# Output projection and skip sums of a decoder layer in products of rounded parts, on one Trainium2 core

## The chip, the cores and the metric

The kernel runs on one core of a Trainium2 chip. The metric is the device time of one execution in microseconds. Three runs of the kernel before took 540.54, 540.75 and 542.11 us: a median of 540.75.

## What is computed

The input is x, 16 sequences of 128 tokens of 256 features in float32. One decoder layer, with a layer norm behind each of its three parts:

```python
x = layernorm(x + attention(x))   # 16 heads of 16, causal in chunks of 64, RMS norm of o per head, then o @ wo.T
x = layernorm(x + xattn(x, ctx))  # kv = x * ctx per pair of channels; long convolution with k,
                                  # y = conv(kv) + kv * skip, out = sum over i of y * ctx
x = layernorm(x + ffn(x))         # gelu(x Wg) * (x Wu), times Wd; the weights are 4-bit codes with scales
```

In attention, q and k are products of two projections each. `skip` is one number for each of the 128 tokens. The FFN is 2048 wide.

## The kernel before

**Groups.** The 16 sequences are four groups of 512 tokens (g = 0 to 3; the text calls them group one to four). What comes before the FFN, called the front here (attention, convolution, skip sum), is cut into stages; the FFN is 16 tiles of 128 rows. After group one's front, which runs alone, the front of group g runs in between the FFN tiles of group g - 1: in slot s an engine does its part of gate of tile s, then the first stages of the slot, then its part of up, the second stages, its part of down, the third stages. TensorE does down one tile late. The fixed lists `slots` (lines 224 to 236) and `last_slots` for group four (lines 238 to 245) say which stage stands where. Between two groups lies a turn (`turn`, one function for each engine), with the end of one front, the start of the next, and the last layer norm of the group before.

**Order.** Each engine runs its own list in the order in which the schedule writes it, and waits on semaphores (`count`, `wait_ge`). A wait at the head of an engine's list holds up everything behind it on that engine.

**Products of parts.** TensorE takes float32 operands in several passes. Most products are therefore made of parts: a value is rounded to float32r by a copy on ScalarE (`_hi`), VectorE subtracts to get the rest (`_lo`), and `split_mm` (lines 155 to 159) makes three single-pass products of them. The float32 products left in the front are the output projection (`outproj`, line 1290), the convolution (lines 1320 to 1323) and the skip sum (line 1339).

**Attention's end.** Slot 5 gives the RMS (`sums`, `rms`); slot 6 ends with ScalarE's `wide` (line 644); slot 7 begins with `factor`: TensorE transposes the factors (line 1278), ScalarE copies them (line 651), VectorE multiplies o by them (line 855). Behind that in slot 7 come, on VectorE, `inner` (line 1099, inter = gelu x up) and `split` (line 1088, inter_lo), and on ScalarE `inner_hi` (line 727) between the two. Slot 8 has both halves of `outproj`, one behind gate, one behind up; VectorE adds each half to x (line 883) and takes the statistics. Slot 9 normalises (line 876) and transposes x1 for the convolution. Group four has the same stages one slot earlier.

**Group two** also has the rest of the weight unpacking beside it (`unpack`, lines 766 to 794 on VectorE, 585 to 598 on ScalarE), a piece ahead of `inner` in each of slots 1 to 5 and 7 to 10.

**Convolution and skip sum.** Sixteen `conv` stages end in slot 15. POOL makes kv (line 533) and the products for the skip sum (`skip_products`, line 501, in conv 12 and 14). VectorE gates and sums each convolution one stage later (`conv_sum`, lines 905, 910). In the turn TensorE makes the two skip sums (line 1339, one matrix product each with `skip_mat`, a block matrix that holds the skip factor), transposes the convolution back (line 1351, after `conv_ready`) and starts the next group's projections, whose tokens are split into parts (`split_x`, lines 564 and 739) at the start of the turn. The loads of tokens stand on SP (line 380).

Of the kernel before, what the change touches and what calls it, by code (L numbers as in the profile page):

```python
# [20 lines left out]
P = 128  # L21
# [32 lines left out]
def decoder_layer(nc, x, xT, ctx, ctxT, wq, wk, wvT, woT, fT, bias, skip, toep,  # L54
# [7 lines left out]
    with ExitStack() as stack:  # L62
# [10 lines left out]
        wo_sb = sb("wo_sb", [P, KT, D])  # L73
# [7 lines left out]
        skip_mat = sb("skip_mat", [P, CH, CI])  # L81
        head_sel = sb("head_sel", [P, HT])
# [8 lines left out]
        with ExitStack() as early:  # L91
            def sbe(name, shape, dt=F32):
                return early.enter_context(nc.sbuf_tensor(name, shape, dt))
            wv_sb = sbe("wv_sb", [P, KT, D])
            xT_sb = sbe("xT_sb", [P, KT, T])
            inter = sbe("inter", [P, 2, T])
        wv_lo = sb("wv_lo", [P, KT, D], F32R)
        xT_lo = sb("xT_lo", [P, KT, T], F32R)
        inter_lo = sb("inter_lo", [P, 2, T], F32R)

# [10 lines left out]
        kT_sb = sb("kT_sb", [P, KT, T])  # L111
# [12 lines left out]
        qbd = sb("qbd", [P, 4, T])  # L124
# [51 lines left out]
        shifted, masked, deq_ready, wlo_ready = sems("shifted", "masked", "deq_ready", "wlo_ready")  # L176
        minus_ready, wlo_mm, wlo_act = sems("minus_ready", "wlo_mm", "wlo_act")
# [9 lines left out]
        last_mm, last_stored = sems("last_mm", "last_stored")  # L187
        end_inter, end_hi, end_lo = sems("end_inter", "end_hi", "end_lo")
# [8 lines left out]
        weight = sb("weight", [P, 2, 2, QC])  # L197
# [33 lines left out]
        slots[7] = [("factor", 0), pause, pause]  # L231
# [327 lines left out]
        def _(act):  # L559
# [20 lines left out]
            act.wait_ge(filled, 6)  # L580
            act.wait_ge(bd_ready, 1)
# [57 lines left out]

            def wide(g, _):  # L640

                count(act, ms_mm, 2, g, 2)
                count(act, rms_ready, 1, g, 1)
                nc.scalar.activation(rms_sb[:].rearrange("p k (n e) -> p (k n) e", e=DK),
                                     inv_rms[:].unsqueeze(2).broadcast_to([P, NB * H, DK]), ACT.Copy)\
                    .then_inc(wide_ready, 1)

            def factor(g, _):
                count(act, rT_mm, 2, g, 2)
                for mt in range(KT):  # L650
                    nc.scalar.activation(by_seq(fac_sb, mt), factor_part(mt), ACT.Copy).then_inc(rT_ready, 1)

# [12 lines left out]
            def conv(g, h):  # L665

                if h + NTOEP - 1 < CH:
                    load_filter(g, h + NTOEP - 1)

# [13 lines left out]
            def turn(done, prev, g, beside=nothing):  # L683
# [8 lines left out]
                if g is not None:  # L692
                    if g:
                        split_x(g)
# [21 lines left out]
            def inner_hi(g, n):  # L716
# [8 lines left out]
                if n >= 2:  # L725
# [4 lines left out]
                                 "norm": norm, "conv": conv},  # L730
# [4 lines left out]
        def _(dve):  # L735
# [26 lines left out]
            dve.wait_ge(const_ready, 4)  # L762
            nc.vector.tensor_scalar(skip_mat[:], skip_mat[:], skip_sb[:, 0:1], None, ALU.mult).then_inc(dve_const, 1)
# [59 lines left out]

            def rms(g, _):
# [26 lines left out]
            def factor(g, _):  # L851
                count(dve, o_mm, NU_S, g, NU_S)
                count(dve, rT_ready, 2, g, 2)
                for mt in range(KT):
                    nc.vector.tensor_tensor(by_seq(o_sb, mt), o_part(mt), by_seq(fac_sb, mt), ALU.mult)\
                        .then_inc(on_ready, 1)

# [32 lines left out]
            def conv(g, h):  # L890

                if h:
                    conv_sum(g, h - 1)
                if g == 0 and h == CH - 1:
# [94 lines left out]
            def turn(done, prev, g, beside=nothing):  # L989
# [8 lines left out]
                if g is not None:  # L998
                    if not isinstance(g, int) or g:
                        split_x(g)  # L1000
# [100 lines left out]
            def finish():  # L1101
# [17 lines left out]
                for b in range(NB):  # L1119
# [3 lines left out]

            schedule(dve, turn, {"score": score, "squares": squares, "rms": rms, "factor": factor, "outproj": outproj, "norm": norm,
                                 "conv": conv, "join": join, "norm2": norm2, "late": late}, nothing, inner, split, unpack, finish)


        @block.tensor
        def _(pe):
# [154 lines left out]
            def outproj(g, j):  # L1284
                if isinstance(g, int) and g == 0:
                    pe.wait_ge(dve_const, 8)
                count(pe, on_ready, 2, g, 2)
                for b in (2 * j, 2 * j + 1):
# [43 lines left out]
            def skip(g, j):  # L1332
# [4 lines left out]
                    elif g == 0 and j:  # L1337
                        pe.wait_ge(z_ready, CH - 1)
                    nc.tensor.matmul(skip_bank(g, j)[:, :], skip_mat[:].rearrange("p h i -> p (h i)"), prod_sb[:, j, :],
# [171 lines left out]
```

## Time and profile before

| | |
|---|---|
| median of three runs | 540.75 us |
| the profiled execution | 540.84 us, its span 539.0 us |
| TensorE busy | 521.3 us, 97% of the span |
| VectorE busy | 369.4 us, 69% |
| ScalarE, POOL busy | 153.2 us (28%), 125.6 us (23%) |
| mean granted TensorE clock | 0.996 |
| chain that ended last | TensorE 84%, VectorE 9%, issue 3% |

Times on the time lines are microseconds from the start of the span. PE is TensorE, PEld its weight loads, DVE VectorE, ACT ScalarE. A row "x8" is several records in one; a float32 product leaves two records. A duration holds the latency, and the next instruction of the engine can start before it is over: the pitch from start to start is what an engine needs for one. A few records are missing. A bracket at the end of a row is the time that the engine sat idle before it, and who ended that.

### The profile page before, as it was taken

To read this page: it belongs to the slowest core of one execution; us is meant where nothing else is said; L and a number is where in the kernel's file an instruction comes from. 1 tells how busy PE (TensorE), PEld (TensorE's weight loads), DVE (VectorE), ACT (ScalarE), POOL (GpSimd) and SP (SyncE) were. 2 spreads that over 40 slices of the span, in tenths; PEclk is the share of its full clock that TensorE was granted. 3 is DMA by queue.
4 is the path that set the end of the run, shared out by engine and by line. 5 is a ranking of instruction groups with operands and counts; after the bars stand their busy time and mean duration, and the time that the engine had idled before them with its cause. 6 is when DMAs were issued, how large, how long until landed. Compare 5 with 4: busy or idle time off the path is not lost.

```text
span 539.0 us, 8767 instructions
## 1 busy us (share of the span) xinstructions
PE 521.3 (97%) x3335; PEld 424.2 (79%) x3335; DVE 369.4 (69%) x774; ACT 153.2 (28%) x277; POOL 125.6 (23%) x194
## 2 busy tenths in 40 slices
PE   8999899899999999999999999999999999999994
PEld 8746676667888888867888888866888888888883
DVE  5998989878595678865454768875464777743335
ACT  4564300333422112331333111241332101333230
POOL 3000198210014452220004444120013570100001
PEclk9999999999999999999999999999999999999998
DMA  5662321401111110050001110040001210010001
GB/s 158 170 184 79 88 78 52 136 21 49 51 29 29 52 49 1 0 193 5 1 1 49 50 50 11 1 152 6 1 1 49 69 40 1 2 39 1 1 0 39
DMA packets 25256, 26.80 MB, mean 50 GB/s; under 512 B 2816, under 2 KB 22784, under 8 KB 25216
## 3 DMA queue, kind: packets, MB, share of 16 engines
q1 hardware_dynamic: 14752, 16.26, 9.8%
q10 hardware_dynamic: 10032, 8.43, 5.4%
q0 software_dynamic: 432, 1.57, 0.8%
q8 instruction: 26, 0.43, 0.3%
q14 instruction: 14, 0.11, 0.1%
HBM read 24.15 MB, written 2.10 MB: 49 GB/s over the span
## 4 chain that ended last, share of the span: by engine, by line
PE 84%; DVE 9%; issue 3%; DMA 1%; POOL 1%; ACT 1%; POOLq 0%; DVEq 0%; SPq 0%; ACTq 0%
PE bank L1157 17%; PE bank L1158 16%; PE bank L1159 16%; PE front_bank L1320 5%; PE front_bank L1323 5%; PE front_bank L1321 5%; PE front_bank L1228 3%; PE front_bank L1214 3%; PE front_bank L1157 2%; PE front_bank L1159 2%; PE front_bank L1158 2%; PE front_bank L1290 2%; DMA raw_s<-in_up_s 1%; PE front_bank L1263 1%; DVE st L864 1%
## 5 line engine op out<-in xcount | busy, mean ns | idle before, releaser
L1157 PE MATMUL bank<-x2T_lo,ffn_hi 128*128 128x512 f32 x256 | 109.7, 429 | 1.4 <-DVE x2T_lo L1043 1.4
L1158 PE MATMUL bank<-x2T_hi,ffn_lo 128*128 128x512 f32 x256 | 100.7, 393 | 0.0
L1159 PE MATMUL bank<-x2T_hi,ffn_hi 128*128 128x512 f32 x256 | 100.7, 393 | 0.0
L1099 DVE TENSOR_TENSOR inter<-bank,inter 128x512 f32<-128x512 f32 x63 | 43.5, 691 | 82.6 <-PE bank L1159 82.4
L533 POOL TENSOR_TENSOR qbd<-qT_sb,ctxT_sb 128x256 f32<-128x256 f32 x128 | 79.4, 643 | 67.5 <-PE front_bank L1323 54.0
L474 POOL TENSOR_TENSOR ve<-ve,minus_half 128x2 f32<-128x2 f32 x24 | 18.4, 766 | 306.9 <-DVE ve L869 248.5
L727 ACT ACTIVATE inter_hi<-inter 128x512 fp32r<-128x512 f32 x63 | 39.8, 632 | 145.5 <-DVE inter L1099 145.5
L1157 PE MATMUL bank<-ffn_lo,inter_hi 128*128 128x256 f32 x256 | 76.3, 298 | 1.2 <-DVE inter_lo L1088 0.9
L714 ACT ACTIVATE inter<-bank 128x512 f32<-128x512 f32 x64 | 38.2, 597 | 128.5 <-PE bank L1159 128.5
L1158 PE MATMUL bank<-ffn_hi,inter_lo 128*128 128x256 f32 x256 | 71.6, 280 | 0.0
L1159 PE MATMUL bank<-ffn_hi,inter_hi 128*128 128x256 f32 x256 | 71.1, 278 | 0.0
L1088 DVE TENSOR_TENSOR inter_lo<-inter,inter_hi 128x512 fp32r<-128x512 f32 x63 | 47.4, 753 | 23.2 <-ACT inter_hi L727 17.5
L1157 PEld LDWEIGHTS bank<-x2T_lo,ffn_hi 128*128 128x128 f32 x256 | 48.1, 188 | 15.6 <-issue 8.0
L1159 PEld LDWEIGHTS bank<-x2T_hi,ffn_hi 128*128 128x128 f32 x256 | 48.1, 188 | 11.1
L1158 PEld LDWEIGHTS bank<-x2T_hi,ffn_lo 128*128 128x128 f32 x256 | 48.3, 189 | 7.8 <-issue 0.2
L814 DVE TENSOR_TENSOR gate_q<-front_bank,causal 128x1024 f32<-128x1024 f32 x32 | 39.1, 1222 | 20.7 <-PE front_bank L1228 20.7
L1157 PEld LDWEIGHTS bank<-ffn_lo,inter_hi 128*128 128x128 f32 x256 | 48.2, 188 | 6.4 <-issue 4.2
L905 DVE TENSOR_TENSOR qbd<-front_bank,ctxT_sb 128x256 f32<-128x256 f32 x128 | 47.8, 415 | 3.7 <-PE front_bank L1323 3.3
L1158 PEld LDWEIGHTS bank<-ffn_hi,inter_lo 128*128 128x128 f32 x256 | 48.1, 188 | 1.8
L1159 PEld LDWEIGHTS bank<-ffn_hi,inter_hi 128*128 128x128 f32 x256 | 48.0, 188 | 0.0
L910 DVE TENSOR_REDUCE gate_q<-qbd 128x64 f32<-128x512 f32 x64 | 43.9, 686 | 2.2
L1320 PE MATMUL front_bank<-qbd,toep_sb 128*128 128x256 f32 x128 | 39.1, 387 | 2.6 <-POOL qbd L533 1.9
(145 smaller groups left out, 775.0 us busy)
## 6 DMA issues: line engine op xcount, KB each, us to landing
toep_sb<-in_toep ACTq DMA_DIRECT2D x64, 128.0 KB, 2.1
xT_sb<-in_xT SPq DMA_DIRECT2D x4, 512.0 KB, 5.5
ctxT_sb<-in_ctxT SPq DMA_DIRECT2D x4, 512.0 KB, 4.8
x_sb<-in_x SPq DMA_DIRECT2D x4, 512.0 KB, 6.0
ctx_sb<-in_ctx SPq DMA_DIRECT2D x4, 512.0 KB, 6.9
out<-ctxT_sb POOLq DMA_DIRECT2D x3, 512.0 KB, 3.4
raw_w<-in_gate_p SPq DMA_DIRECT2D x8, 128.0 KB
raw_s<-in_gate_s SPq DMA_DIRECT2D x8, 128.0 KB
```

The source lines that it names most:

```text
L533: nc.gpsimd.tensor_tensor(pairs(kv_sb, h % 2)[:, kt], v_i, c_j, ALU.mult).then_inc(kv_ready, 1)
L714: nc.scalar.activation(inter[:, n % 2, :], gate_ps[:, :], ACT.Gelu_apprx_tanh).then_inc(gelu_ready, 1)
L727: nc.scalar.activation(inter_hi[:, n % 2, :], inter[:, n % 2, :], ACT.Copy).then_inc(ihi_ready, 1)
L814: nc.vector.tensor_tensor(sc_sb.rearrange("p (r k) c -> p r k c", k=2), front_ps[:, :, 0:2 * P].rearrange("p r (k c) -> p r k c", c=P), ca ...
L905: last = nc.vector.tensor_tensor(pairs(z_sb, h % 2)[:, lt], fb[h % 2][:, :].rearrange("p (k b j i) -> p k b j i", k=KT, b=NB, i=CI)[:, lt] ...
L910: nc.vector.tensor_reduce(conv_sb[:, :, :, h * CI:(h + 1) * CI], pairs(z_sb, h % 2), AX.X, ALU.add)\
L1088: nc.vector.tensor_tensor(inter_lo[:, n % 2, :], inter[:, n % 2, :], inter_hi[:, n % 2, :].bitcast(F32), ALU.subtract).then_inc(ilo_ready, 1)
L1099: nc.vector.tensor_tensor(inter[:, n % 2, :], up_ps[:, :], inter[:, n % 2, :], ALU.mult).then_inc(inter_ready, 1)
L1157: nc.tensor.matmul(ps, w_hi, x_lo, start=start, stop=False, skip_group_check=True)
L1158: nc.tensor.matmul(ps, w_lo, x_hi, start=False, stop=False, skip_group_check=True)
L1159: return nc.tensor.matmul(ps, w_hi, x_hi, start=False, stop=stop, skip_group_check=True)
L1320: nc.tensor.matmul(fb[h % 2][:, 0:n], diag, kv[:, 0:n], start=True, stop=True)
```

## The change

1. In groups two to four, `outproj` uses three single-pass products of parts for each float32 product. wo is split once: ScalarE rounds it at the end of slot 6 of group two, ahead of `wide`, and VectorE subtracts in slot 7. o is split for each group: ScalarE's `round_o` stands in slot 7 behind up, VectorE's `split_o` in slot 7 behind down. TensorE waits for both halves of o_lo (and once for wo_lo).
2. In groups two and three each skip sum is two single-pass products with a matrix of ones and zeros (`skip_ones`, rounded once at the start). ScalarE scales by skip and rounds (`prod_hi`) in conv 13 and 15, VectorE makes `prod_lo` there.
3. The tokens of groups three and four are split within the slots and not in the turn: ScalarE's half behind the factor copies of slot 7, VectorE's half behind the second half of `outproj` in slot 8.
4. Tiles are laid out anew to make room: o_hi and o_lo lie over qbd, wo_lo over wo_sb, prod_lo over kT_sb, prod_hi over weight.

```diff
@@ -70,7 +70,7 @@
         wv_hi = sb("wv_hi", [P, KT, D], F32R)
-        wo_sb = sb("wo_sb", [P, KT, D])
+        wo_hi = sb("wo_hi", [P, KT, D], F32R)
         ffn_hi = sb("ffn_hi", [P, 3, 2, F], F32R)
@@ -79,6 +79,7 @@
         skip_mat = sb("skip_mat", [P, CH, CI])
+        skip_ones = sb("skip_ones", [P, P], F32R)
         head_sel = sb("head_sel", [P, HT])
@@ -94,9 +95,17 @@
             inter = sbe("inter", [P, 2, T])
+            wo_sb = sbe("wo_sb", [P, KT, D])
+            qbd = sbe("qbd", [P, 4, T])
+            kT_sb = sbe("kT_sb", [P, KT, T])
+            weight = sbe("weight", [P, 2, 2, QC])
         wv_lo = sb("wv_lo", [P, KT, D], F32R)
         inter_lo = sb("inter_lo", [P, 2, T], F32R)
+        wo_lo = sb("wo_lo", [P, KT, D], F32R)
+        o_parts = sb("o_parts", [P, 4, T], F32R)
+        prod_lo = sb("prod_lo", [P, 2, T], F32R)
+        prod_hi = sb("prod_hi", [P, 2, T], F32R)
@@ -108,7 +117,6 @@
         rms_sb = x1T_sb = qT_sb
-        kT_sb = sb("kT_sb", [P, KT, T])
         fac_sb = prod_sb = kT_sb
@@ -121,7 +129,7 @@
-        qbd = sb("qbd", [P, 4, T])
+        o_hi, o_lo = o_parts[:, 0:2, :], o_parts[:, 2:4, :]
         q_two = qbd[:].rearrange("p u (k c) -> p u k c", c=S)
...
@@ -194,7 +204,6 @@
         code_f16 = code[:].bitcast(F16)[:, :, 1::2]
-        weight = sb("weight", [P, 2, 2, QC])
         x2T_hi = sb("x2T_hi", [P, 2, T], F32R)
@@ -228,7 +237,7 @@
         slots[6] = [pause, pause, ("wide", 0)]
-        slots[7] = [("factor", 0), pause, pause]
+        slots[7] = [("factor", 0), ("round_o", 0), ("split_o", 0)]
         slots[8] = [("outproj", 0), ("outproj", 1), pause]
@@ -578,6 +587,9 @@
             act.wait_ge(filled, 6)
+            act.wait_ge(const_ready, 2)
+            nc.scalar.activation(skip_ones[:], skip_mat[:].rearrange("p h i -> p (h i)"), ACT.Copy)\
+                .then_inc(ones_rounded, 1)
             act.wait_ge(bd_ready, 1)
@@ -637,8 +649,18 @@
+            def round_o(g, _):
+
+                if g:
+                    for mt in range(KT):
+                        count(act, on_ready, 2, g, mt + 1)
+                        nc.scalar.activation(o_hi[:, mt, :], o_sb[:, mt, :], ACT.Copy).then_inc(ohi_ready, 1)
+
             def wide(g, _):
+                if g == 1:
+                    act.wait_ge(wo_mm, 2)
+                    nc.scalar.activation(wo_hi[:], wo_sb[:], ACT.Copy).then_inc(wohi_ready, 1)
                 count(act, ms_mm, 2, g, 2)
@@ -649,6 +671,8 @@
                     nc.scalar.activation(by_seq(fac_sb, mt), factor_part(mt), ACT.Copy).then_inc(rT_ready, 1)
+                if 0 < g < G - 1:
+                    split_x(g + 1)
@@ -666,6 +690,13 @@
                     load_filter(g, h + NTOEP - 1)
+                if 0 < g < G - 1 and h in (CH - 3, CH - 1):
+                    j = h // 2 + 2 - CH // 2
+                    count(act, prod_ready, 2, g, j + 1)
+                    if j == 0:
+                        act.wait_ge(wlo_ready, NU - NU_S)
+                    nc.scalar.activation(prod_hi[:, j, :], prod_sb[:, j, :], ACT.Copy, scale=skip_sb[:, 0:1])\
+                        .then_inc(phi_ready, 1)
@@ -690,8 +721,6 @@
                 if g is not None:
-                    if g:
-                        split_x(g)
                     for p in range(0, 8, 2):
...
@@ -760,6 +789,7 @@
             dve.wait_ge(const_ready, 4)
+            dve.wait_ge(ones_rounded, 1)
             nc.vector.tensor_scalar(skip_mat[:], skip_mat[:], skip_sb[:, 0:1], None, ALU.mult).then_inc(dve_const, 1)
@@ -821,6 +851,12 @@
+            def outproj_of(g, j):
+
+                outproj(g, j)
+                if j and 0 < g < G - 1:
+                    split_x(g + 1)
+
             def rms(g, _):
@@ -855,6 +891,18 @@
+            def split_o(g, _):
+
+                if g == 1:
+                    dve.wait_ge(wohi_ready, 1)
+                    nc.vector.tensor_tensor(wo_lo[:], wo_sb[:], wo_hi[:].bitcast(F32), ALU.subtract)\
+                        .then_inc(wolo_ready, 1)
+                if g:
+                    for mt in range(KT):
+                        count(dve, ohi_ready, 2, g - 1, mt + 1)
+                        nc.vector.tensor_tensor(o_lo[:, mt, :], o_sb[:, mt, :], o_hi[:, mt, :].bitcast(F32),
+                                                ALU.subtract).then_inc(olo_ready, 1)
+
             def stats(g, ln, tile, j):
@@ -891,6 +939,12 @@
                     conv_sum(g, h - 1)
+                if 0 < g < G - 1 and h in (CH - 3, CH - 1):
+                    j = h // 2 + 2 - CH // 2
+                    count(dve, phi_ready, 2, g - 1, j + 1)
+                    nc.vector.scalar_tensor_tensor(prod_lo[:, j, :], prod_sb[:, j, :], skip_sb[:, 0:1],
+                                                   prod_hi[:, j, :].bitcast(F32), ALU.mult, ALU.subtract)\
+                        .then_inc(plo_ready, 1)
                 if g == 0 and h == CH - 1:
@@ -995,9 +1049,6 @@
                     conv_sum(prev, CH - 1)
-                if g is not None:
-                    if not isinstance(g, int) or g:
-                        split_x(g)
                 if done is not None:
...
@@ -1285,6 +1336,17 @@
                 count(pe, on_ready, 2, g, 2)
+                if g == 1:
+                    pe.wait_ge(wolo_ready, 1)
+                if g:
+                    count(pe, olo_ready, 2, g - 1, 2)
+                    for b in (2 * j, 2 * j + 1):
+                        toks = slice(b * S, (b + 1) * S)
+                        for kt in range(KT):
+                            last = split_mm(fb[j][:, (b % 2) * D:(b % 2 + 1) * D], o_hi[:, kt, toks], o_lo[:, kt, toks],
+                                            wo_hi[:, kt, :], wo_lo[:, kt, :], kt == 0, kt == KT - 1)
+                    last.then_inc(wo_mm, 1)
+                    return
                 for b in (2 * j, 2 * j + 1):
@@ -1336,6 +1398,13 @@
                         pe.wait_ge(z_ready, CH - 1)
+                    if 0 < g < G - 1:
+
+                        count(pe, plo_ready, 2, g - 1, j + 1)
+                        nc.tensor.matmul(skip_bank(g, j)[:, :], skip_ones[:], prod_hi[:, j, :], start=True, stop=False)
+                        nc.tensor.matmul(skip_bank(g, j)[:, :], skip_ones[:], prod_lo[:, j, :], start=False, stop=True)\
+                            .then_inc(skip_mm, 1)
+                        return
                     nc.tensor.matmul(skip_bank(g, j)[:, :], skip_mat[:].rearrange("p h i -> p (h i)"), prod_sb[:, j, :],
```

## Rows read from the trace of the kernel before

**Rows 1.** The page: busy time by engine; costliest groups (busy us, mean ns, idle before).

```profile
PE 521.3 (97%) x3335; PEld 424.2 (79%) x3335; DVE 369.4 (69%) x774; ACT 153.2 (28%) x277; POOL 125.6 (23%) x194
...
L1157 PEld LDWEIGHTS bank<-ffn_lo,inter_hi 128*128 128x128 f32 x256 | 48.2, 188 | 6.4 <-issue 4.2
```

**Rows 2.** TensorE's waits, whole run: releaser: us in total, times, longest us.

```profile
PE front_bank L1320 <- POOL qbd L533: 1.9, 2, 1.5
...
PE front_bank L1157 <- DVE xT_lo L739: 0.3, 1, 0.3
```

**Rows 3.** TensorE's time line, group three's output projection: start, us, engine, line, instruction.

```profile
275.81 1.89 PE L1290 MATMUL front_bank<-wo_sb,gate_q 128*128 128x256 f32 x8
...
277.76 0.39 PE L1158 MATMUL bank<-x2T_hi,ffn_lo 128*128 128x512 f32 x1
...
282.06 0.39 PE L1157 MATMUL bank<-x2T_lo,ffn_hi 128*128 128x512 f32 x1
...
284.85 0.28 PE L1157 MATMUL bank<-ffn_lo,inter_hi 128*128 128x256 f32 x1
...
286.24 1.04 PE L1302 MATMUL front_bank<-ident,x_sb 128*128 128x128 f32 x8
```

**Rows 4.** Time lines of TensorE, VectorE, ScalarE and POOL, turn behind group two's front.

```profile
210.36 1.88 PE L1339 MATMUL bank<-kT_sb,skip_mat 128*128 128x512 f32 x4
212.08 1.04 PE L1351 MATMUL front_bank<-ident,gate_q 128*128 128x128 f32 x8
...
209.14 0.76 DVE L905 TENSOR_TENSOR qbd<-front_bank,ctxT_sb 128x256 f32<-128x256 f32 x2
...
210.53 1.28 DVE L739 TENSOR_TENSOR xT_lo<-xT_sb,xT_hi 128x512 fp32r<-128x512 f32 x2
...
206.41 1.14 ACT L564 ACTIVATE xT_hi<-xT_sb 128x512 fp32r<-128x512 f32 x2
...
204.97 1.27 POOL L501 TENSOR_TENSOR kT_sb<-x_sb,ctx_sb 128x512 f32<-128x512 f32 x1
```

**Rows 5.** Time lines of ScalarE, TensorE and VectorE, slots 6 to 9, group two.

```profile
144.49 1.04 ACT L644 ACTIVATE qT_sb<-inv_rms 128x1024 f32<-128x1024 f32 x1
145.80 1.04 PE L1278 MATMUL front_bank<-ident,qT_sb 128*128 128x128 f32 x8
...
150.83 1.89 PE L1290 MATMUL front_bank<-wo_sb,gate_q 128*128 128x256 f32 x8
...
160.79 0.36 PE L1157 MATMUL bank<-ffn_lo,inter_hi 128*128 128x256 f32 x1 [0.75 <-DVE inter_lo L1088]
...
152.81 0.69 DVE L1088 TENSOR_TENSOR inter_lo<-inter,inter_hi 128x512 fp32r<-128x512 f32 x1 [0.69 <-ACT inter_hi L727]
153.42 0.68 DVE L883 TENSOR_TENSOR x_sb<-front_bank,x_sb 128x512 f32<-128x512 f32 x1
...
155.29 0.51 DVE L774 TENSOR_SCALAR code<-raw_w 128x256 int32<-128x256 int32 x2
...
159.95 0.69 DVE L1088 TENSOR_TENSOR inter_lo<-inter,inter_hi 128x512 fp32r<-128x512 f32 x1
```

**Rows 6.** Time lines of VectorE and ScalarE, slot 7, group three.

```profile
273.03 1.29 DVE L855 TENSOR_TENSOR gate_q<-front_bank,kT_sb 128x512 f32<-128x512 f32 x2 [2.75 <-ACT kT_sb L651]
...
275.62 0.69 DVE L1088 TENSOR_TENSOR inter_lo<-inter,inter_hi 128x512 fp32r<-128x512 f32 x1 [0.70 <-ACT inter_hi L727]
...
274.96 0.63 ACT L727 ACTIVATE inter_hi<-inter 128x512 fp32r<-128x512 f32 x1 [2.02 <-DVE inter L1099]
```

**Rows 7.** Stretch behind group two's projection: busy us, PEclk after POOL's count, DMA, GB/s.

```profile
151.00:157.00 6.00, 6.00 (x34) 5.33 (x34) 5.07 (x14) 1.64 (x3) 0.69 (x1) 1.00 0.00 0
```

**Rows 8.** Time lines of ScalarE and VectorE at the start, of SP's token loads.

```profile
9.85 0.31 ACT L583 ACTIVATE minus_ident<-ident 128x128 fp32r<-128x128 f32 x1
...
10.87 0.28 DVE L763 TENSOR_SCALAR skip_mat<-skip_mat,skip_sb 128x128 f32<-128x128 f32 x1
...
134.17 0.40 SPq L380 DMA_DIRECT2D xT_sb<-in_xT  x1
```

More of the change, by code:

```diff
@@ L176, in decoder_layer @@
         shifted, masked, deq_ready, wlo_ready = sems("shifted", "masked", "deq_ready", "wlo_ready")
+        wohi_ready, wolo_ready, ohi_ready, olo_ready = sems("wohi_ready", "wolo_ready", "ohi_ready", "olo_ready")
         minus_ready, wlo_mm, wlo_act = sems("minus_ready", "wlo_mm", "wlo_act")
@@ L187, in decoder_layer @@
         last_mm, last_stored = sems("last_mm", "last_stored")
+        ones_rounded, phi_ready, plo_ready = sems("ones_rounded", "phi_ready", "plo_ready")
         end_inter, end_hi, end_lo = sems("end_inter", "end_hi", "end_lo")
@@ L729, in _ @@
             schedule(act, turn, {"score": score, "squares": squares, "wide": wide, "factor": factor, "x1T": x1T,
-                                 "norm": norm, "conv": conv},
+                                 "norm": norm, "conv": conv, "round_o": round_o},
                      gelu, inner_hi, nothing, unpack, nothing)
@@ L1122, in finish @@
                                             ALU.subtract, ALU.mult).then_inc(res_ready, 1)
-            schedule(dve, turn, {"score": score, "squares": squares, "rms": rms, "factor": factor, "outproj": outproj, "norm": norm,
-                                 "conv": conv, "join": join, "norm2": norm2, "late": late}, nothing, inner, split, unpack, finish)
+            schedule(dve, turn, {"score": score, "squares": squares, "rms": rms, "factor": factor, "outproj": outproj_of, "norm": norm,
+                                 "conv": conv, "split_o": split_o, "join": join, "norm2": norm2, "late": late}, nothing, inner, split, unpack, finish)
         @block.tensor
```

## The prediction

> **What bounds the kernel now.** I read the page's busy table first: TensorE is busy for 521.3 of 539.0 us, the next engine for 369.4 [rows 1]. Then who TensorE waited for: the list is short, its longest single wait 1.5 us [rows 2], and the same view cut to 164 to 410 us, where most of the changed work lies, lists none. So between those times each microsecond that the change takes out of TensorE's stream shortens the run, and each that TensorE is made to wait lengthens it; nothing gives it back, since TensorE has no idle time to catch up in. The one wait within reach of the change is 0.75 us at 160.79 in group two, where VectorE, not TensorE, is the last to finish: it works without a gap from 153.42 to 159.95 us, in 14 entries, up to the tile that TensorE waits for [rows 5]. Third, the time line around the output projection and the turns, which gives the slack that the new roundings have.
>
> **TensorE's own work.** A half of the output projection (four float32 products of 256 columns) starts at 275.81; the second product behind it starts at 277.76, and one such product takes 0.23, so the half takes 1.72. Twelve single-pass products of 256 columns run from 284.85 to 286.24: 1.39 [rows 3]. The new half is twelve of these: 0.33 less. The Trainium skill (TensorE: Matmul & The Clock Gate, part 3, "What overlaps and what doesn't") says that a weight load overlaps products in flight only when the row groups differ; by that rule each product here would pay its load too, 0.12 + 0.19, a new half would take 3.7 against 1.72 + 8 x 0.19 = 3.2, and the sum below would come to 549.6. The rows contradict it, so it gets no chance: the load takes 188 ns, yet products start every 0.116 us, so it is hidden [rows 1, 3].
>
> Both skip sums of a group take 210.36 to 212.08, 1.72 us [rows 4]. Four single-pass products of 512 columns replace them; twelve take 282.06 to 284.85, so one 0.2325 and four 0.93 [rows 3]. That is 0.79 less per turn, in two turns (groups two and three). Of it some 0.05 is lost: the second prod_lo stands on VectorE before the last conv_sum. Now that conv_sum starts at 209.14; prod_lo's price lies between the pitch of a subtraction, 0.60 (two take 1.28, one 0.69), and its whole duration, 0.69 [rows 4, 5]; at 0.61 plus its 0.05 handover conv_sum ends near 211.3, where TensorE now wants it at 210.36 + 0.93 = 211.29. I take 0.74 per turn, bounds 0.6 and 0.79: **-1.5** in all. The first prod_lo waits for ScalarE, and ScalarE for POOL's product; POOL's second product is done at 206.24, ScalarE comes to it at 206.41 [rows 4], and the first stands one stage earlier, in VectorE's idle time before it multiplies the last FFN tile. Queued behind that ScalarE wait is inter_hi of the tile, and nobody is later for it.
>
> **The new chain in front of the output projection.** In slot 7 ScalarE's queue holds gelu, the factor copies (and now split_x of the next group), inner_hi, then round_o; VectorE's holds the factor products, inner, split, then split_o. So the rounding of o is queued behind inner_hi, though o itself has long been ready. Group three: inner_hi starts at 274.96; a 512-column copy to float32r has a pitch of 0.54 (two take 1.14, one about 0.6 [rows 4]), so o_hi 1 ends at 274.96 + 0.54 + 1.14 = 276.64. VectorE's split starts at 275.62, o_lo 0 at 276.23, and o_lo 1 runs from 276.84 to 277.53 [rows 6]. TensorE is there at 275.81 [rows 3] and now waits until about 277.56: **1.75 us**. Taking off two shorter halves (0.66), group three loses **1.1**. Is it made worse later? From 277.56 TensorE has two halves of 1.39 and four FFN parts of 1.39 up to down(8), at 285.90. VectorE starts the second sum at 277.56 + 3 x 1.39 + 0.2 = 281.93, takes 1.87 with its statistics (153.42 to 155.29 in [rows 5]), 1.2 for the moved split of tokens, and 0.69 for split: 285.7. The margin is 0.2, so the moved VectorE split costs nothing; if that cover were gone, up to its 1.2 us would be paid. Its ScalarE half (1.14 behind the factor copies) ends before 274.96, where inner_hi has to wait for VectorE anyway. Group four has the same order without split_x and the same gaps before inner_hi: again **1.1**, bounds 0.8 and 1.4 for both, from margins of 0.2 to 0.3.
>
> **Group two** is dearer, as VectorE also unpacks weights there. First, wo is rounded on ScalarE in front of wide: wide starts at 144.49 and takes 1.04, TensorE's transposes start at 145.80 [rows 5], so 0.27 of its 0.54 is covered and 0.3 is paid; all that follows in this chain is later by 0.3. VectorE's split starts at 152.81 + 0.3; behind it now stand wo_lo and two o_lo instead of the residual sum (pitches 0.61, 0.60, 0.60, the last 0.68): ready at 155.63. TensorE, there at 150.83 + 0.3, waits 4.5 us. Its half and the drain take 1.6, so VectorE's residual sum starts at 157.25 instead of 153.42. From there its queue has the same work as before up to split of tile 8 (sum and statistics, a piece of unpacking, inner, the second sum; no gap, 153.42 to 159.95), plus the moved split of tokens, 1.2. Split of tile 8 starts at 157.25 + 6.53 + 1.2 = 164.98 instead of 159.95. TensorE waited for just that tile at 160.79 [rows 5], so its next step moves by **+5.0**; that replaces the shorter halves, which fall into its waits. Bounds: 3.8 if the VectorE backlog were not what decides (4.5 less 0.66), 5.6 if each of ten handovers adds 0.06.
>
> **What costs nothing.** skip_ones is one more small copy on ScalarE at 9.85 + 0.31, before VectorE scales the matrix at 10.87 [rows 8]. In the turns TensorE doesn't wait for the old splits of tokens [rows 2], so moving them gains nothing. No DMA is added or moved past anything on SP, and nothing is added on POOL; the tokens of group three are issued at 134.17 [rows 8], 14 us before the new reader at about 148; for group four the gap is wider.
>
> **Sum.** The profiled execution took 540.84 us (span 539.0), 0.09 over the median of 540.75. +5.0 + 1.1 + 1.1 - 1.5 = +5.7, so 546.5. About 0.3%, 1.6 us, is what a measurement of this kernel can tell from no change.
>
> **Rivals.** (1) *The roundings are hidden*, and only the shorter products are left: 6 x 0.33 + 1.5 = 3.5 less, 537.3. For it: o is ready at 273.03 + 1.29 = 274.32 in group three [rows 6]; with a copy of 0.63 [rows 6] and a subtraction of 0.68 behind the second product it would be split at 275.7, before TensorE's 275.81. It decides whether round_o starts before inner_hi. Against: the queue's order as written. Chance 0.07.
> (2) *The clock falls.* Group two's wait of 4.5 us is three times the longest TensorE wait in the trace, 1.5 [rows 2], and all stretches around it stand at a granted 1.00, the 2.4 GHz level [rows 7]. If it fell to 1.2 GHz behind that wait, the half of 1.39 would take 2.8, VectorE's chain would start 1.4 later, and with two halves so 2.1: 547.9 to 548.6. The Trainium skill names such idle gaps between bursts of products as what makes the clock fall (the same page, "Why this matters for your kernels"); no wait of the trace is long enough to bear that out or deny it. Chance 0.12.
> (3) *Gains and waits cancel*: that needs group two to lose no more than about 1 us, so that wo_lo and the split of tokens would lie in gaps of VectorE; its gapless row speaks against that. 541, chance 0.04.
> (4) *Group two loses only TensorE's own wait*, 3.8, and groups three and four 0.8 each: 540.84 + 3.8 + 1.6 - 1.5 = 544.7. Chance 0.12. The forecast keeps 0.65.
>
> **Numbers.** 546.5. The range goes from 544.0, under rival 4 with skips at their best, to 549.0, over rival 2. It leaves out rivals 1 and 3 and some overshoot. Faster by over 0.3%: rival 1, 0.07; within: rival 3 and the low end of rival 4, 0.05; slower: 0.88.
>
> **What would show it.** Right: TensorE's list of waits names o_lo in front of the output projection, three times, about 4.5, 1.75 and 1.75 us, and inter_lo of group two with more than 0.7; the skip products take 0.93 per turn. Wrong: no wait on o_lo (rival 1), a granted clock under 1.00 behind group two's wait (rival 2), or new waits on prod_lo or in the turns, for which I have no price. If conv(0) of any group comes late because x1T does, my margins of 0.2 were too thin.

## The result: 1.4% slower, and the profile after

The changed kernel takes 548.95 us (median of 5 runs, 548.64 to 549.71) where the kernel before took 541.57 in the runs beside it (5 runs, 540.54 to 542.11). The ratio is 1.0142, with a 95% interval of 1.0132 to 1.0153. The sign and the places of the loss are those of the forecast, the amount is not: 548.95 against 546.5, at the upper end of the range. The profiled execution took 548.64, 7.8 above that of before.

The page of the changed kernel: TensorE is as busy as before within 0.4 us [rows 1], in a span longer by 7.8. So nearly all of the loss is time in which TensorE waits; and as its busy time did not fall although the products got shorter, some products seem to have run slower. (The last row is the granted clock in tenths, one digit for each of 40 slices of 13.7 us; its two first 8s stand at 41 to 55 and at 150 to 164 us.)

```profile
span 546.8 us, 8852 instructions
...
PE 521.7 (95%) x3359; PEld 425.3 (78%) x3359; DVE 376.3 (69%) x785; ACT 159.5 (29%) x289; POOL 126.4 (23%) x194
...
PEclk9998999999989999999999999999999999999998
```

TensorE's list of waits, the view of [rows 2], has one new entry, the first below. The third has grown: before, these waits for inter_lo were 0.9 us in two, the longest 0.7. The second is as it was [rows 2].

```profile
PE front_bank L1208 <- DVE o_parts L903: 7.9, 3, 4.5
PE front_bank L1382 <- POOL qbd L542: 1.9, 2, 1.5
PE bank L1208 <- DVE inter_lo L1139: 1.6, 2, 1.4
```

Three waits of 7.9 us in all stand in front of the output projection (predicted: 4.5, 1.75 and 1.75, together 8.0), and at tile 8 of group two TensorE waits 1.40 instead of 0.75 [rows 5]. Its time line in group two shows the wait of 4.46 and that of 1.40 one behind the other:

```profile
146.27 1.09 PE L1329 MATMUL front_bank<-ident,qT_sb 128*128 128x128 f32 x8
...
155.98 0.55 PE L1208 MATMUL front_bank<-wo_lo,o_parts 128*128 128x256 f32 x1 [4.46 <-DVE o_parts L903]
156.33 0.41 PE L1209 MATMUL front_bank<-wo_hi,o_parts 128*128 128x256 f32 x1
156.54 0.41 PE L1210 MATMUL front_bank<-wo_hi,o_parts 128*128 128x256 f32 x1
...
158.68 0.59 PE L1208 MATMUL bank<-x2T_lo,ffn_hi 128*128 128x512 f32 x1
...
167.48 0.36 PE L1208 MATMUL bank<-ffn_lo,inter_hi 128*128 128x256 f32 x1 [1.40 <-DVE inter_lo L1139]
...
168.97 1.04 PE L1364 MATMUL front_bank<-ident,x_sb 128*128 128x128 f32 x8
```

The transposes start at 146.27, 0.47 later than before [rows 5]. TensorE then waits 4.46 us. The half that follows runs from 155.98 to the next FFN part at 158.68: 2.70 us, where 1.39 was forecast. Its products have a pitch of 0.21 us (156.33 to 156.54), where 0.116 stood before [rows 3]. The windows of that stretch say why; the last three columns are the granted clock, the DMA share and GB/s:

```profile
core 0: us, PE busy (x) PEld busy (x) DVE busy (x) ACT busy (x) POOL busy (x), PEclk, DMA share, GB/s
150.00:153.00 3.00, 1.52 (x8) 0.92 (x6) 2.51 (x6) 0.36 (x2) 0.00 (x0) 1.00 0.00 0
153.00:156.00 3.00, 0.02 (x1) 0.05 (x1) 2.50 (x4) 2.35 (x5) 0.00 (x0) 0.95 0.00 0
156.00:159.00 3.00, 3.00 (x13) 3.00 (x14) 0.08 (x1) 0.00 (x0) 0.00 (x0) 0.50 0.00 0
159.00:162.00 3.00, 3.00 (x21) 2.68 (x21) 2.90 (x10) 0.00 (x0) 0.69 (x1) 0.98 0.00 0
```

The clock stood at 1.00 up to 153, fell shortly before 156 (0.95 over those three us) while TensorE waited, and was at 0.50 (the lower of its levels, 1.2 GHz) from 156 to 159. Before, it was 1.00 here [rows 7]. VectorE's time line of the same stretch:

```profile
153.34 0.69 DVE L1139 TENSOR_TENSOR inter_lo<-inter,inter_hi 128x512 fp32r<-128x512 f32 x1 [0.70 <-ACT inter_hi L756]
153.95 0.68 DVE L898 TENSOR_TENSOR wo_lo<-wo_sb,wo_hi 128x512 fp32r<-128x512 f32 x1
154.55 1.29 DVE L903 TENSOR_TENSOR o_parts<-gate_q,o_parts 128x512 fp32r<-128x512 f32 x2
158.92 0.69 DVE L931 TENSOR_TENSOR x_sb<-front_bank,x_sb 128x512 f32<-128x512 f32 x1 [3.08 <-PE front_bank L1210]
...
165.45 1.29 DVE L768 TENSOR_TENSOR xT_lo<-xT_sb,xT_hi 128x512 fp32r<-128x512 f32 x2
166.65 0.68 DVE L1139 TENSOR_TENSOR inter_lo<-inter,inter_hi 128x512 fp32r<-128x512 f32 x1
```

VectorE's queue is the predicted one: split, wo_lo, two o_lo, and only then the residual sum. The sum starts at 158.92 instead of the predicted 157.25. From there to the split of tile 8 (166.65) it is 7.73 us, and the forecast had 6.53 + 1.2 = 7.73. In group three the waits are near the forecast and the clock stays up:

```profile
283.65 0.36 PE L1208 MATMUL front_bank<-wo_lo,o_parts 128*128 128x256 f32 x1 [1.70 <-DVE o_parts L903]
...
285.14 0.39 PE L1208 MATMUL bank<-x2T_lo,ffn_hi 128*128 128x512 f32 x1
...
286.51 0.28 PE L1208 MATMUL front_bank<-wo_lo,o_parts 128*128 128x256 f32 x1
...
287.93 0.28 PE L1208 MATMUL bank<-ffn_lo,inter_hi 128*128 128x256 f32 x1
...
293.51 0.71 PE L1364 MATMUL front_bank<-ident,x_sb 128*128 128x128 f32 x5
```

And the two skip sums in the turn behind group two:

```profile
217.03 0.39 PE L1404 MATMUL bank<-prod_hi,skip_ones 128*128 128x512 f32 x1
...
217.98 1.09 PE L1420 MATMUL front_bank<-ident,gate_q 128*128 128x128 f32 x8
```

They take 0.95 us, from 217.03 to the transposes at 217.98, against 1.72 before [rows 4].

To place the difference I cut both profiles at the same three events of TensorE and subtract: a group's first per-head sums (`sums`, slot 5), its transposes of x1 (slot 9), and the transposes of the tokens near the end of the turn behind it. A row called a turn thus holds the group's convolution as well.

| stretch | before, us | after, us | difference | forecast |
|---|---|---|---|---|
| group two, sums to x1 | 135.66 to 162.29 | 135.82 to 168.97 | +6.5 | +5.0 |
| turn behind group two | 162.29 to 225.58 | 168.97 to 231.59 | -0.67 | -0.74 |
| group three | 260.64 to 286.24 | 266.62 to 293.51 | +1.29 | +1.1 |
| turn behind group three | 286.24 to 349.51 | 293.51 to 356.14 | -0.64 | -0.74 |
| group four | 380.42 to 406.01 | 387.04 to 413.93 | +1.30 | +1.1 |

These make +7.8 of the 7.8. At the end of group one's turn the changed kernel is 0.14 later, and about as much is given back in what the rows leave out.

### The profile page after: what moved, and what is told of

The parts are those of the page before. It is cut to its first block, busy times and chain, and to the rows that moved or that the text cites. A ratio compares the mean times of both kernels' runs of the same rounds, so it can differ in the third digit from the quotient of the medians.

```text
span 546.8 us, 8852 instructions
## 1 busy us (share of the span) xinstructions
PE 521.7 (95%) x3359; PEld 425.3 (78%) x3359; DVE 376.3 (69%) x785; ACT 159.5 (29%) x289; POOL 126.4 (23%) x194
## 4 chain that ended last, share of the span: by engine, by line
PE 82%; DVE 9%; issue 3%; ACT 2%; DMA 1%; POOL 1%; POOLq 0%; DVEq 0%; SPq 0%; ACTq 0%
PE bank L1208 16%; PE bank L1209 15%; PE bank L1210 15%; PE front_bank L1382 5%; PE front_bank L1385 5%; PE front_bank L1383 5%; PE front_bank L1279 3%; PE front_bank L1265 3%; PE front_bank L1208 3%; PE front_bank L1210 3%; PE front_bank L1209 3%; DMA raw_s<-in_up_s 1%; PE front_bank L1314 1%; DVE st L912 1%; PE bank L1302 1%
## 5 line engine op out<-in xcount | busy, mean ns | idle before, releaser
L542 POOL TENSOR_TENSOR qbd<-qT_sb,ctxT_sb 128x256 f32<-128x256 f32 x128 | 80.5, 651 | 68.9 <-PE front_bank L1385 54.0
```

Source lines behind the costliest of these rows:

```text
L542: nc.gpsimd.tensor_tensor(pairs(kv_sb, h % 2)[:, kt], v_i, c_j, ALU.mult).then_inc(kv_ready, 1)
```

## Experiments

Three theories are told apart. **W**: TensorE waits because round_o stands behind inner_hi in ScalarE's queue, and split_o and the split of tokens stand in front of VectorE's work for tile 8; put them elsewhere and the loss goes. Against it stand readings by which the loss stays whatever the order, or doesn't hang on the output projection. **C**: the part of group two's loss that the forecast lacks is the clock. **H** is the prediction's own view of the turns: the shorter skip sums pay by themselves, and moving the split of tokens out of the turn does nothing. Kernels of the first four experiments were timed beside runs of the kernel before with a median of 541.39 us, those of the last four beside 541.17.

**1. early_round: the order alone.** Of the changed kernel, only the places of two stages are moved: o is rounded and split as soon as it is there.

```diff
-        slots[7] = [("factor", 0), ("round_o", 0), ("split_o", 0)]
+        slots[7] = [("factor", 0), pause, pause]
...
             def factor(g, _):      # ScalarE, behind the factor copies, ahead of split_x
+                round_o(g, 0)
...
             def factor(g, _):      # VectorE, behind the factor products
+                split_o(g, 0)
```

> The change with only its order altered: o is rounded on ScalarE right behind the factor copies and split on VectorE right behind the factor products, ahead of inner. Theory W (the loss is TensorE waiting for o_lo because the rounding is queued behind inner_hi): no wait on o_lo in groups three and four, so each gains 0.66 where it lost 1.3; in group two VectorE's own queue stays long (wo_lo, two o_lo, unpacking, the moved token split), its tile 8 comes 3.4 us later than in the kernel before; with 1.3 back from the skip sums the whole is 0.8 us over the kernel before, near 542.4. Rival D (the parts themselves are dear, wherever they are made): stays within 1 us of the change, near 549.

Measured: 542.93 us (9 runs), ratio 1.0024 [1.0014, 1.0033]. Waits on o_lo shrink from 7.9 us to one of 0.3, but group two still waits for VectorE:

```profile
152.11 0.35 PE L1210 MATMUL front_bank<-wo_lo,o_parts 128*128 128x256 f32 x1 [0.31 <-DVE o_parts L905]
...
154.88 0.47 PE L1210 MATMUL bank<-x2T_lo,ffn_hi 128*128 128x512 f32 x1 [1.11 <-DVE inter L1152]
...
164.58 0.36 PE L1210 MATMUL bank<-ffn_lo,inter_hi 128*128 128x256 f32 x1 [2.09 <-DVE inter_lo L1141]
```

Group two now costs 3.3 us more than before (136.11 to 166.07), group three is 0.46 shorter than before (263.72 to 288.86) and group four 0.48 (382.37 to 407.48). So W holds: the same arithmetic, in another order, gives back 6 of the 7.4 us. Some of that is the clock, which stays at 1.00 here where it fell in the change (experiment 5 has its price). What is left sits in group two: wo_lo and o_lo now stand in front of VectorE's inner of slot 7 (the wait of 1.11), the split of tokens still in front of its work for tile 8 (the wait of 2.09).

**2. no_outproj: parts 2 and 3 without part 1.** Output projection in float32 in all groups; skip sums and split of tokens as in the change.

```diff
-        slots[7] = [("factor", 0), ("round_o", 0), ("split_o", 0)]
+        slots[7] = [("factor", 0), pause, pause]
...
-                if g == 1:
-                    act.wait_ge(wo_mm, 2)
-                    nc.scalar.activation(wo_hi[:], wo_sb[:], ACT.Copy).then_inc(wohi_ready, 1)
...
-                if g:
+                if False:           # outproj on TensorE: three products of parts
```

> The change without its first part: the output projection stays in float32 in all groups; skip sums in parts and moved token splits stay. Theory W: the skip sums give back 0.65 us per turn, the moved token split costs 1.2 us in group two, where VectorE has no gap, and nothing in group three: 541.5, within 0.3 of the kernel before. Rival D2 (moved token splits and skip parts carry much of the loss): 544 or more.

Measured: 542.61 us (11 runs, 541.69 to 543.53), ratio 1.0023 [1.0013, 1.0033]. In its profile group two costs 1.2 more than before (136.58 to 164.39), the turns 0.68 and 0.62 less (62.61 and 62.65 us, read as in the table), groups three and four the same: +1.2 - 1.3, nothing in sum. The profiled run is 0.9 over that of before, because its clock fell once in group one (69 to 72 us; the last section has the price). The median is 1.2 over the runs beside it, where nothing was expected, and the clock does not explain that: six runs at a mean clock of 0.994 took 541.69 to 542.61, three at 0.995 took 542.68 to 542.90. What does stays open.

**3. tokens_only: part 3 alone.** As no_outproj, and the skip sums as before too.

```diff
-                if 0 < g < G - 1 and h in (CH - 3, CH - 1):
+                if False:           # prod_hi on ScalarE, prod_lo on VectorE
...
-                    if 0 < g < G - 1:
+                    if False:       # the products with skip_ones
```

> The third part alone: tokens of groups three and four split within the slots, output projection and skip sums as before. Theory W: TensorE's wait for tile 8 of group two grows from 0.75 to 1.95 us, +1.2, and nothing else changes: 542.8. Rival F (VectorE catches up, the move is free): 541.6. Rival G (the turns were bound by VectorE, the move gains): under 541.

Measured: 544.54 us (6 runs, 542.0 to 545.36), ratio 1.0052 [1.0033, 1.0072]. The wait is where W has it, on tile 8 of group two:

```profile
161.84 0.35 PE L1205 MATMUL bank<-ffn_lo,inter_hi 128*128 128x256 f32 x1 [1.92 <-DVE inter_lo L1136]
```

It is 1.92 us where 0.75 stood before [rows 5]: the 1.2 of the moved subtraction, in full. But group two costs 2.2 more than before (135.53 to 164.34) and the turn behind it 0.5 more (164.34 to 228.16), and the median is 1.7 above what was expected. The windows around that wait (same columns as above) show where the rest went in the profiled run: the clock fell right behind it.

```profile
159.00:162.00 3.00, 1.08 (x5) 0.59 (x5) 2.93 (x10) 0.80 (x2) 1.06 (x1) 1.00 0.42 131
162.00:165.00 3.00, 3.00 (x16) 3.00 (x16) 2.30 (x7) 0.63 (x1) 0.00 (x0) 0.51 0.00 0
165.00:168.00 3.00, 3.00 (x16) 2.60 (x15) 1.18 (x2) 1.69 (x3) 1.37 (x3) 0.92 0.00 0
```

Whether the longer wait brought the fall about is not shown: early_round waits 2.09 us at the same place and keeps 1.00. The one of the six runs with a mean granted clock of 0.997 took 542.0 us; the others, at 0.990 to 0.994, took 543.57 or more. The turn behind group three takes 63.28 (288.88 to 352.16), as before: alone, moving the split out of it gains nothing.

**4. skips_only: part 2 alone.** The split of tokens goes back into the turn, the output projection to float32.

```diff
-                if 0 < g < G - 1:
-                    split_x(g + 1)      # slot 7, ScalarE
...
+                    if g:
+                        split_x(g)      # the turn, ScalarE
...
-                if j and 0 < g < G - 1:
-                    split_x(g + 1)      # slot 8, VectorE
...
+                if g is not None:
+                    if not isinstance(g, int) or g:
+                        split_x(g)      # the turn, VectorE
```

> The second part alone: skip sums of groups two and three in parts, tokens split in the turn as before. Theory W with a detail: prod_lo puts 0.6 us more in front of VectorE's work in the turn, TensorE's fourth projection waits for VectorE's q there, and the 0.79 us saved is lost again: 0.3 to 0.4 us worse per turn, 542.3. Rival H (the turn is TensorE's alone, as the prediction took it): 1.5 us better, 540.1.

Measured: 543.10 us (7 runs), ratio 1.0031 [1.002, 1.0043]: slower than before, with less work for TensorE. H falls. TensorE's list of waits has an entry that neither kernel has:

```profile
PE front_bank L1206 <- DVE qT_sb L832: 2.0, 2, 1.0
```

It is one us in each of two turns, and VectorE's time line in the turn behind group two shows what stands in front of it:

```profile
211.40 1.28 DVE L765 TENSOR_TENSOR xT_lo<-xT_sb,xT_hi 128x512 fp32r<-128x512 f32 x2
212.60 1.28 DVE L1033 TENSOR_TENSOR ctxT_sb<-bank,x_sb 128x512 f32<-128x512 f32 x2
...
217.01 0.75 DVE L832 SCALAR_TENSOR_TENSOR qT_sb<-front_bank,b_small,gate_q 128x512 f32<-128x512 f32 x1
```

The split of tokens (211.40) takes 1.2 of VectorE's time ahead of the q that TensorE waits for (217.01), and the second prod_lo stands ahead of it too. Each turn is 63.8 us against 63.3 before: the 0.78 saved at the skip sums is lost again and 0.5 with it, 1.0 of that in this wait. With the split moved out, as in the change, a turn is 62.6. So beside part 2, part 3 is worth 1.2 a turn, 2.4 in all, and costs 1.2 in group two (experiment 3).

**5. keep_warm: the wait filled.** The changed kernel with 17 products that nobody reads, issued into a spare bank while TensorE waits for o_lo in group two.

```diff
+                if g == 1 and j == 0:
+                    for _ in range(17):
+                        nc.tensor.matmul(fb[2][:, :], fold_hi[:, 0, 0, 0:P],
+                                         fold_hi[:, 0].rearrange("p k n -> p (k n)"),
+                                         start=True, stop=True, skip_group_check=True)
```

> The change with one thing added: in group two TensorE fills its wait in front of the output projection with 17 products of 512 columns into a free bank, read by nobody (17 x 0.23 = 3.9 us of a 4.5 us wait). Theory C (the idle wait lets the clock fall, and the first half of the projection then takes 2.70 instead of 1.39): the granted clock stays 1.00 around the wait, the half takes 1.39, and the whole is 1.3 us under the change, near 547.6. Rival (the half is slow because of its operands, or the clock falls with other things): clock and time stay as in the change, near 549.

Measured: 547.79 us (4 runs), ratio 1.0123 [1.0108, 1.0138]: below the changed kernel by 1.2 in the medians and by 1.0 in the ratios, whose intervals still overlap, so the profile has to decide. The windows and the time line of the same stretch:

```profile
153.00:156.00 3.00, 2.53 (x12) 1.76 (x10) 2.50 (x4) 2.50 (x5) 0.00 (x0) 1.00 0.00 0
156.00:159.00 3.00, 2.87 (x18) 2.65 (x19) 1.14 (x3) 0.00 (x0) 0.00 (x0) 1.00 0.00 0
```

```profile
151.51 4.02 PE L1341 MATMUL front_bank<-fold_hi 128*128 128x512 f32 x17
156.13 0.35 PE L1208 MATMUL front_bank<-wo_lo,o_parts 128*128 128x256 f32 x1 [0.60 <-DVE o_parts L903]
...
157.63 0.39 PE L1208 MATMUL bank<-x2T_lo,ffn_hi 128*128 128x512 f32 x1
```

o_lo comes no earlier (156.13 against 155.98), but the clock stays at 1.00 and the half takes 1.50 instead of 2.70. Group two costs 5.27 (135.97 to 167.87) instead of 6.5. In all four runs the mean granted clock is 0.996 or 0.997; in the five of the changed kernel it is 0.989 or 0.992. C holds, and its price is 1.25 us.

**6. outproj_only: part 1 alone**, skip sums and split of tokens as before (the edits of skips_only and tokens_only together, with the output projection left as in the change).

> The first part alone: output projection in parts as in the change; skip sums in float32, tokens split in the turn. Theory W: group two loses 5.3 (6.5 less the 1.2 of the moved token split), groups three and four 1.3 each: 7.9 over the kernel before, 549.3, as much as the whole change. Rival (the moved token split is hidden in group two once VectorE's chain is that long): 550.3 or more.

Measured: 549.49 us (4 runs), ratio 1.0156 [1.0141, 1.0170]. So the output projection carries the whole loss; parts 2 and 3, beside it, take at most a little off (the intervals overlap). Its wait of 4.47 is followed by the same slow half (157.20 to 159.83, 2.63; granted clock 0.50 from 158 to 160):

```profile
157.20 0.49 PE L1209 MATMUL front_bank<-wo_lo,o_parts 128*128 128x256 f32 x1 [4.47 <-DVE o_parts L901]
...
159.83 0.63 PE L1209 MATMUL bank<-x2T_lo,ffn_hi 128*128 128x512 f32 x1
```

**7. rearranged: all three parts in another order.** As early_round, and beyond that wo is rounded on ScalarE behind the second squares of group two and subtracted on VectorE at the end of slot 6 (not shown); the split of tokens goes to the start of the convolution; and the second pieces of FFN weights, which VectorE unpacks in slots 7 to 9, go to slots 11 to 13.

```diff
-        SECOND = [(0, 1, 0) if 1 <= s <= 10 and s != 6 else (0, 0, 0) for s in range(NT)]
+        SECOND = [(0, 1, 0) if s in (1, 2, 3, 4, 5, 10, 11, 12, 13) else (0, 0, 0) for s in range(NT)]
...
             def squares(g, mt):
+                if g == 1 and mt == KT - 1:
+                    act.wait_ge(wo_mm, 2)
+                    nc.scalar.activation(wo_hi[:], wo_sb[:], ACT.Copy).then_inc(wohi_ready, 1)
...
             def conv(g, h):        # ScalarE and VectorE
+                if h == 0 and 0 < g < G - 1:
+                    split_x(g + 1)
```

> All parts of the change, in another order: o rounded and split right behind the factor products; wo rounded behind the squares of group two and split in VectorE's gap at the end of slot 6; tokens split at the first convolution; the unpacking of slots 7 to 9 of group two moved to slots 11 to 13, where VectorE idles 2.2 us before inner. Theory W: no wait on o_lo, none for tile 8 of group two (0.75 in the kernel before); 1.2 us gained in group two, 0.5 in three and four each, 0.65 in two turns: 3.4 under the kernel before, 538.0. Rival D: within 1 us of the kernel before, or over it.

Measured: 537.68 us (6 runs, 537.01 to 538.45), ratio 0.9937 [0.9923, 0.9951]: faster than either kernel. There is no wait on o_lo or on tile 8. In group three, the time line of ScalarE, then of VectorE, then of TensorE:

```profile
272.74 1.23 ACT L660 ACTIVATE o_parts<-gate_q 128x512 fp32r<-128x512 f32 x2 [0.83 <-DVE gate_q L890]
```

```profile
273.41 1.30 DVE L906 TENSOR_TENSOR o_parts<-gate_q,o_parts 128x512 fp32r<-128x512 f32 x2
274.62 0.69 DVE L1155 TENSOR_TENSOR inter<-bank,inter 128x512 f32<-128x512 f32 x1
```

```profile
274.85 0.36 PE L1213 MATMUL front_bank<-wo_lo,o_parts 128*128 128x256 f32 x1
...
276.34 0.41 PE L1213 MATMUL bank<-x2T_lo,ffn_hi 128*128 128x512 f32 x1
...
277.75 0.28 PE L1213 MATMUL front_bank<-wo_lo,o_parts 128*128 128x256 f32 x1
...
279.17 0.28 PE L1213 MATMUL bank<-ffn_lo,inter_hi 128*128 128x256 f32 x1
```

o_lo is done at 274.71 and TensorE is there at 274.85: this is rival 1 of the prediction, with its own condition met (round_o starts before inner_hi). Groups two to four take 1.5, 0.48 and 0.48 less than before, each turn 0.67 less. What each of the moves gives by itself was not run.

**8. rearranged_f32: the same without part 1**, so that the products of parts are priced by themselves.

> The same order without the first part: output projection in float32, skip sums in parts, tokens split at the first convolution, unpacking moved. Theory W: 0.75 gained in group two and 0.65 in two turns: 2.0 under the kernel before, 539.4; the 1.4 between this and the kernel with all parts is what the single-pass output projection is worth. Rival: no difference between the two, or this one the faster.

Measured: 539.66 us (10 runs), ratio 0.9973 [0.9962, 0.9983]. Its groups take 25.62 each against 25.1 with the products of parts: 0.5 a group, 1.5 in all by the profiles. The medians differ by 2.0, but by 1.6 to 1.7 where runs of like clock are compared (0.992 to 0.995, and 0.996 to 0.998). So the arithmetic of part 1 is worth 1.5 to 2 us in the right place; in the place that the change gave it, it cost 8 (experiment 6).

## Why the prediction was right in its places and wrong in its sum

**Right: the waits, their cause and their sizes.** The three waits on o_lo are listed with 4.46, 1.70 and 1.70 us against 4.5, 1.75 and 1.75. The list counts from the end of the product in front, 0.39 after its start, where the prediction counts from the moment at which the next could have started, 0.23 after it; counted so they are 0.16 longer, 4.62 and 1.86. And early_round showed the cause, the places of round_o and split_o behind inner_hi and split. The backlog that decides group two measured 7.73 us against 6.53 + 1.2, and tokens_only showed the 1.2 alone (1.92 against 0.75). Rounding wo ahead of wide cost 0.31 (0.47 less the 0.16 by which group two starts late), against 0.3. Rival 4 (TensorE's own wait alone) falls: tile 8 waits longer than before, not shorter. Rival 3 falls with it.

**The step that failed: the sum's term for group two, +5.0, took the half behind the long wait at full clock.** The term measured +6.5, and 1.25 of the difference is the clock, which stood in a rival at 0.12 and was left out of the sum. The prediction's own rival 2 describes what happened: the clock fell in the wait of 4.5 us, the half took 2.70 (the rival said 2.8), and VectorE's chain, which begins at that half's end, started 1.24 later than in keep_warm, counted from the sums (the rival said 1.4). That its upper time, 548.6, is nearly the profiled run's 548.64 is luck: it stands for two slow halves, and only the first was slow (the second, 160.28 to 161.69, took 1.41). For one the rival said 547.9, and the sizes below made up the rest. The Trainium skill (TensorE: Matmul & The Clock Gate, "Why this matters for your kernels") had said that such a gap drops the clock, and in group two the trace agrees with it: 0.50 from 156 to 159 us, and 1.00 in keep_warm. I gave it little because no wait of the trace before was long enough to bear it out. That was lack of evidence read as evidence against: the trace does not cover a wait three times as long as any in it, and the only statement on it pointed one way. It should have been the forecast.

**Sizes that were off, of the terms of the sum.** (a) The new half was taken at 1.39, the pitch of a run of products in midstream. The halves of group three measure 1.49 (283.65 to 285.14) and 1.42 (286.51 to 287.93): the first product of the first half has a pitch of 0.20, not 0.117, and 0.19 in rearranged (274.85 to 275.04), where nothing is waited for; that of the second half has 0.12 (286.51 to 286.63), so it is not every switch of operands that costs this. And the first half starts 1.86 us later against the sums than it did before, where 1.75 was forecast. With both, group three's 1.1 becomes 1.86 less 0.23 and 0.30, 1.33 against the 1.29 measured; group four has the same +1.30. Keep_warm's group two exceeds 5.0 by 0.27, of which its half of 1.50 is 0.11 and the longer wait of 4.62 is 0.12. (b) The skip pair took 0.95 against 0.93, and a turn won 0.65 instead of 0.74: up to the transposes behind the skip sums 0.78 was won, 0.11 of it lost again by the end of the turn. (c) The 549.6 that the prediction gives for weight loads that are not hidden counts groups three and four alone; by the same reckoning VectorE's chain in group two would start 2.3 later as well. The halves of 1.49 and 1.42 rule those loads out either way.

**Wrong, though it did not show in the sum:** "moving them gains nothing" of the split of tokens. It holds for that move alone, as tokens_only shows; but VectorE's slack in the turn was smaller than what the skip sums save there, and without the move skips_only loses 0.5 a turn where 0.74 was to be won. The two parts cannot be costed one by one.

By terms, of the 2.1 us between the forecast and the profiled run: clock 1.25, the rest of group two 0.27, groups three and four 0.4, turns 0.2.

## What to carry to other kernels

Where a stage is split in two across engines, look at what stands in front of each half in its own queue: here a copy that could start 13.1 us behind the sums (259.62 to 272.74 in rearranged) started 14.9 behind them (266.62 to 281.48 in the change), after one that depends on another engine, and moving it was worth more than the arithmetic. Price a new long wait on TensorE with a slower clock behind it, and with whoever waits for the slowed products. And when a part shortens one engine's share of a stretch, ask for the next engine's slack there before calling another part free.

## What the hardware showed that was not expected

The clock also fell where no long wait stood before it. In tokens_only it fell behind a wait of 1.92 us (0.51 from 162 to 165), while early_round waited 2.09 us at the same place and kept 1.00, and both turns' waits of 1.0 in skips_only passed without a fall. In the changed kernel's profile it fell in group one as well. The windows there, with the columns as above:

```profile
47.00:49.00 2.00, 1.93 (x13) 1.40 (x12) 1.90 (x5) 1.54 (x3) 0.00 (x0) 1.00 0.30 78
49.00:51.00 2.00, 2.00 (x13) 1.81 (x13) 1.24 (x6) 0.00 (x0) 0.00 (x0) 0.72 0.32 90
51.00:53.00 2.00, 2.00 (x6) 1.56 (x5) 1.73 (x9) 0.00 (x0) 0.00 (x0) 0.50 0.10 30
```

The time line shows no wait of TensorE from 40 to 53 us, and the profile of before keeps 1.00 over the same work. Such falls of 3 to 4 us stand in group one of four of the ten profiles: at 50 to 54 us here and in outproj_only, at 69 to 73 us in no_outproj and rearranged. Every profile, that of before too, has its last microseconds at 0.50. The Trainium skill (TensorE: Matmul & The Clock Gate, "Why this matters for your kernels") ties the fall to idle gaps between bursts of products; by the runs here a fall can follow a wait of 1.92 us in one kernel and stay away behind one of 2.09 in another. What sets off the falls in group one stays open: the first two have no wait in front of them, the other two begin 0.7 and 0.9 us behind one of 1.5 us, which the other eight profiles have too, without a fall.

From group one's first sums to group two's it is 87.28 us before, and up to 87.35 in the other five profiles without such a fall. With it the stretch is 87.74 here and 87.79 in outproj_only, so the fall costs about 0.5, as TensorE waits 0.9 less for VectorE behind it; in no_outproj and rearranged it is 88.69 and 88.80, and the fall costs 1.4 and 1.5.

It need not be the change that brings such falls about. The kernel before seems to have them in some of its runs: of its 22 runs beside the first four experiments ten have a mean granted clock of 0.996 or 0.997 and twelve one of 0.993 or 0.994, and 3.4 us at 0.50 out of 540 (an estimate from the fall at 162 to 165.5 in tokens_only) lower the mean by 0.003.
